# Attention with 16 heads: spread maxima in a PSUM bank, one K evicted amid the scores, low halves of the weighted sums on GpSimd

## The reference

```python
B, Tt, D = hidden_states.shape        # 32, 112, 512
scale = HEAD_DIM ** (-0.5)            # HEADS = 16, HEAD_DIM = 32
a = _layer_norm(audio_kv, ln_gamma, ln_beta)
Q = (hidden_states @ Wq.T).reshape(B, Tt, HEADS, HEAD_DIM).transpose(0, 2, 1, 3)
K = (a @ Wk.T).reshape(B, Ta, HEADS, HEAD_DIM).transpose(0, 2, 1, 3)
V = (a @ Wv.T).reshape(B, Ta, HEADS, HEAD_DIM).transpose(0, 2, 1, 3)
scores = jnp.einsum('bhtd,bhsd->bhts', Q, K) * scale
scores = jnp.where(mask, scores, jnp.float32(-jnp.inf))
attn = jax.nn.softmax(scores, axis=-1)
out = jnp.einsum('bhts,bhsd->bhtd', attn, V)
out = out.transpose(0, 2, 1, 3).reshape(B, Tt, D) @ Wo.T
return hidden_states + jnp.tanh(gate) * out
```

## Time and profile before

| | us |
|---|---|
| runs: lowest, median, highest | 1032.9, 1038.71, 1041.41 |
| the profiled execution | 1042.68 |
| its span, first to last instruction | 1040.9 |
| busy: PE / PEld / DVE / ACT / POOL | 963.9 / 823.3 / 939.4 / 698.5 / 635.5 |
| mean granted TensorE clock | 0.970 |

### The profile page before, as it was taken

How to read it: one execution, slowest core, us unless ns; L and a number is a source line. 1 busy time by engine, 2 the same in 40 slices (tenths; PEclk the granted TensorE clock), 3 DMA queues, 4 the chain that set the end, 5 groups by cost and what they waited for, 6 DMA issues and landing times.

```text
span 1040.9 us, 26655 instructions
## 1 busy us (share of the span) xinstructions
PE 963.9 (93%) x10687; PEld 823.3 (79%) x10687; DVE 939.4 (90%) x1446; ACT 698.5 (67%) x1299; POOL 635.5 (61%) x665
## 2 busy tenths in 40 slices
PE   8999999999999999999999999999999999999956
PEld 7888877778787787787878877887787877878744
DVE  6852799999999999999999999999999999999997
ACT  2422767777767777677776777776777777776662
POOL 0943456667666666566766667565676666665554
PEclk9999999999999999999999999999999999999988
DMA  9971333233443344323343334423344433433101
GB/s 293 328 245 72 77 86 80 59 80 100 103 103 83 88 103 101 96 65 93 100 104 103 86 85 100 103 78 89 88 101 102 103 83 89 100 96 81 35 20 52
DMA packets 85851, 105.54 MB, mean 101 GB/s; under 512 B 22528, under 2 KB 63488, under 8 KB 85728
## 3 DMA queue, kind: packets, MB, share of 16 engines
q1 hardware_dynamic: 85152, 102.93, 37.5%
q10 hardware_dynamic: 576, 0.92, 0.3%
HBM read 86.39 MB, written 17.43 MB: 100 GB/s over the span
## 4 chain that ended last, share of the span: by engine, by line
DVE 57%; PE 20%; ACT 10%; issue 10%; DMA 2%; POOL 1%; SPq 0%; ACTq 0%; DVEq 0%; POOLq 0%
DVE shared_q L837 25%; DVE rmax L827 13%; PE banks L931 12%; ACT shared_q L607 7%; DVE spread L818 6%; PE banks L954 5%; DVE top L815 3%; PE banks L1086 2%; DVE spread L847 2%; DVE stats L754 2%; DVE dsum L842 2%; DVE shared_r L856 2%; ACT shared_q L616 1%; DMA shared_q<-in_wvT 1%; ACT shared_f L657 1%
## 5 line engine op out<-in xcount | busy, mean ns | idle before, releaser
L837 DVE TENSOR_TENSOR shared_q<-shared_q,spread 125x448 f32<-125x448 f32 x384 | 359.3, 989 | 4.4
L931 PE MATMUL banks<-shared_r,w_k 128*128 128x376 f32 x1536 | 314.1, 356 | 51.8 <-ACT shared_f L621 51.4
L931 PEld LDWEIGHTS banks<-shared_r,w_k 128*128 128x128 f32 x1536 | 274.7, 198 | 79.6 <-ACT shared_f L621 70.8
L474 POOL TENSOR_TENSOR shared_f<-shared_q 125x448 f32<-125x448 f32 x126 | 160.6, 1275 | 240.3 <-PE banks L1092 219.1
L616 ACT ACTIVATE shared_q<-shared_q 125x448 f32<-125x448 f32 x384 | 209.3, 575 | 122.9 <-DVE shared_q L837 122.6
L931 PE MATMUL banks<-w_v,shared_r 128*125 128x512 f32 x1152 | 288.2, 399 | 0.0
L931 PEld LDWEIGHTS banks<-w_v,shared_r 128*125 128x125 f32 x1152 | 218.1, 190 | 45.9
L607 ACT ACTIVATE shared_q<-banks,maskT,rstd 125x448 f32<-125x448 f32 x384 | 242.8, 728 | 1.9 <-PE banks L1073 1.9
L827 DVE TRANSPOSE_TENSOR_REDUCE rmax<-shared_q 128x14 f32<-128x448 f32 x384 | 210.1, 606 | 24.0 <-ACT shared_q L607 23.4
L478 POOL TENSOR_TENSOR shared_f<-shared_f,shared_q 125x448 f32<-125x448 f32 x126 | 170.3, 1352 | 9.9
L454 POOL TENSOR_TENSOR shared_r<-cn,shared_r 128x375 fp32r<-128x375 f32 x124 | 124.6, 1026 | 72.9 <-ACT shared_r L563 72.9
(11 more groups left out here) (92 smaller groups left out, 743.2 us busy)
## 6 DMA issues: line engine op xcount, KB each, us to landing
cn<-in_ctxT SPq DMA_DIRECT2D x128, 187.5 KB, 3.7
rows<-in_ctx SPq DMA_DIRECT2D x32, 720.0 KB
xy<-in_x SPq DMA_DIRECT2D x32, 224.0 KB, 7.2
q_kept<-shared_q SPq DMA_DIRECT2D x8, 896.0 KB, 5.5
shared_q<-q_kept SPq DMA_DIRECT2D x32, 224.0 KB, 3.9
out<-xy SPq DMA_DIRECT2D x32, 224.0 KB, 3.6
shared_f<-in_xT SPq DMA_DIRECT2D x7, 896.0 KB, 11.2
x<-row_stats SPq DMA_DIRECT2D x64, 84.0 KB
```

The lines of the kernel that those rows point to most:

```text
L474: pool.tensor_tensor(psum[0:SP_, h, :], prob[0:SP_, q, 0, :], prob[0:SP_, q, 1, :], ALU.add).then_inc(sum_half, 1)
L837: dve.tensor_tensor(prob[0:SP_, p % NB, j, :], prob[0:SP_, p % NB, j, :], spread[0:SP_, :], ALU.subtract).then_inc(sub_done, 1)
L931: last = pe.matmul(dst, l, m, start=(start and k == 0), stop=(stop and k == len(pairs) - 1))
```

## The change

Three things are changed, and what they need.

1. `spread`, 448 columns in SBUF, becomes the first 448 columns of PSUM bank 0, one of the banks of the scores. The transpose of the maxima (now L834) writes there and the subtraction (now L853) reads one input from SBUF and one from the bank. The reciprocals get a buffer of their own in SBUF, `rspread`, which also serves the maxima of the last pair but one. Since the scores of a pair overwrite bank 0, the scores of an even slot n now wait also until the subtractions of all slots up to n - 3 are done. In the tail the sums move to other banks.
2. ACT evicts K of slot 2m + 2 between the scores of slot 2m and those of slot 2m + 1, no more behind both.
3. The low half of the weighted sums is formed by POOL, behind the chunk sums of its turn, no more by DVE at the start of its turn.

```diff
-        spread = sb("spread", [128, HT])
+        rspread = sb("rspread", [128, HT])
...
+        spread = bank[0][:, 0:HT]
-        last_bank = {2: (bank[2], bank[3]), 3: (bank[4], bank[5])}
+        last_bank = {2: (bank[3], bank[4]), 3: (bank[5], bank[1])}
...
@@ gpsimd
+            def low_half(b):
+                pool.wait_ge(o_hi, b + 1)
+                pool.tensor_tensor(oT[:, 1, :, :].rearrange("p c t -> p (c t)"),
+                                  pv[:, b % 2 * HT:b % 2 * HT + HT],
+                                  oT[:, 0, :, :].rearrange("p c t -> p (c t)").bitcast(F32),
+                                  ALU.subtract).then_inc(o_done, 1)
...
                     sum_chunks(2 * m - 3)
+                if odd and c > 1:
+                    low_half(c - 2)
...
             result(B - 3)
+            low_half(B - 2)
             add_bias(B - 2)
...
@@ scalar
                     scores_out(2 * m)
+                if pair(m + 1):
+                    k_out(2 * m + 2)
                 if m == PAIRS - 1:
                     exponential(SLOTS - 3)
                 if pair(m):
                     scores_out(2 * m + 1)
                 if pair(m + 1):
-                    k_out(2 * m + 2)
                     first_out(m + 1)
...
@@ vector
+            def maxima_of(p):
+                return rspread[:, :] if p // 2 == PAIRS - 2 else spread
...
-                dve.transpose(spread[:, :].rearrange("p (k a) -> p k a", a=32),
+                dve.transpose(maxima_of(p).rearrange("p (k a) -> p k a", a=32),
                               top[:, :].unsqueeze(2).to_broadcast([128, BLK, 32])) \
                     .then_inc(spread_done, 1)
...
-                                      spread[0:SP_, :], ALU.subtract).then_inc(sub_done, 1)
+                                      maxima_of(p)[0:SP_, :], ALU.subtract).then_inc(sub_done, 1)
...
-                if odd and c > 1:
-                    low_half(c - 2)
                 if odd and c + 2 < B and c + 2 > 2:
                     statistics(c + 2)
...
             normalise(B - 2)
-            low_half(B - 2)
             without_maximum(SLOTS - 2)
...
@@ tensor
                 if n % 2 == 0:
                     need(pe, s_out, n * ST)
+                    need(pe, sub_done, (n - 2) * ST)
...
-            weighted_sums(SLOTS - 6, bank[0])
+            weighted_sums(SLOTS - 6, bank[1])
...
-            weighted_sums(SLOTS - 4, bank[1])
+            weighted_sums(SLOTS - 4, bank[2])
             output(B - 2, B * ST)
             last_weighted_sums(SLOTS - 2)
+            pe.wait_ge(pv_out, SLOTS - KT)
             last_weighted_sums(SLOTS - 1)
```

More of the change, by code:

```diff
@@ L713, in _ @@
             v_out(B - 1, 2)
-            weighted_out(SLOTS - 6, 0)
+            weighted_out(SLOTS - 6, 1)
             gated_out(B - 3, KB)
             high_half(B - 2)
-            weighted_out(SLOTS - 4, 1)
+            weighted_out(SLOTS - 4, 2)
             exponential(SLOTS - 2)
@@ L846, in normalise @@
                 dve.wait_ge(rden_done, b + 1)
-                dve.transpose(spread[:, :].rearrange("p (k a) -> p k a", a=32),
+                dve.transpose(rspread[:, :].rearrange("p (k a) -> p k a", a=32),
                               rden[:, :].unsqueeze(2).to_broadcast([128, BLK, 32])) \
@@ L851, in normalise @@
                 o = pv[:, b % 2 * HT:b % 2 * HT + HT]
[L852 to L859, removed]
+                dve.tensor_tensor(o, o, rspread[:, :], ALU.mult).then_inc(o_norm, 1)
             def last_divide(k):
```

## The result

The changed kernel takes 960.0 us (median of four runs, 958.6 to 962.5), the kernel before beside it 1036.7 (the 1038.7 of the table above is the median of three of these four runs). The ratio is 0.926, 95% interval 0.921 to 0.931: 7.4% faster. The profiled execution took 960.5 us.

What follows compares the result with a forecast made beforehand. DVE (95% busy) and PE (94%) were taken as nearly full, PE's floor limiting the gain. From 1042.7 us, 52 for the steady part (14.41 to 13.55 a pair) and 5 at the end gave 985.7; named 985, range 965 to 1015.

Steps and rivals of the forecast that it cites:

- 1.70 us for three with a bank: DVE's subtractions: three take 1.70 us with maxima in PSUM, giving back 131 us of DVE in the steady part.
- the low half at nothing in the steady part: Low half moved from DVE to POOL: costed at nothing in the steady part; 40 us if POOL's cover were gone.
- the loop at 12.8 us: Steady loop from a pair's scores through ACT and DVE to its last subtraction: 12.8 us, against PE's return at 12.91.
- the end at 5 us: Kernel's end, last subtractions and pair 63's exponentials: 5 us gained, bounds 2 and 8.
- The sum's middle part, the new wait: PE's scores wait for DVE's subtractions of two pairs before; loop nearly ties with PE, 0.3 us a pair lost.
- The 65 ns estimated from the Trainium skill: DVE subtractions reading PSUM: each 65 ns dearer, 0.4 us a pair, making the sum about 15 us more.
- PE's floor: PE's steady pace without its wait for the K eviction: 13.25 us a pair, trusted to 0.1 us.
- second derivation: PE's pace from the timeline: 12.91 us at full clock plus 0.43 for half-clock stretches, 13.34 a pair.
- PE's granted clock as before, 0.97: Expected sign in the changed kernel's profile: PE's clock stays 0.97; were it lower, the floor would be wrong.
- The 0.3 us for the tie: Loss from delays where DVE's 12.8 us loop nearly equals PE's 12.91: 0.3 us a pair, between 0 and 0.6.
- PE's floor is reached: Rival for the steady part: PE sets the pace, 13.25 us a pair, 967 us in all; chance 0.12.
- The slower rival: Subtractions stay contended, so the new wait rules the loop: 14.8 us a pair, 1067 us; chance 0.08.

Runs made afterwards that it cites:

- kout_alone: The kernel before with only the K eviction moved between the two slots' scores; 998.9 us, ratio 0.962.
- after_sbuf: The changed kernel with the spread maxima in an SBUF buffer of their own, the new wait of the scores kept; 1123.3 us, ratio 1.076.
- before_fill: The kernel before with eight useless matmuls on PE ahead of each batch's first V projection from batch 3 on; 1021.1 us beside 1041.4, ratio 0.979.
- before_fill2: The kernel before with two useless matmuls on PE ahead of each batch's first V projection from batch 3 on; 1007.9 us beside 1037.9, ratio 0.974.
- after_stall3: The changed kernel with PE waiting, before even pairs' second K projection from pair 6 on, until the first slot's first tile is subtracted; 1052.0 us.
- after_stall2: The changed kernel with PE waiting for DVE's spread maxima before every pair's second K projection from pair 6 on; 1060.4 us.

## Why the prediction was wrong

**Right.** Both engines nearly full, the subtraction's second SBUF input as what POOL and DVE hinder one another by, 1.70 us for three with a bank (1.68), the transpose into a bank at the old price (660 ns for 645, 0.01 us), the low half at nothing in the steady part, the loop at 12.8 us (12.75), the end at 5 us (5.6). That the early K covers most of PE's wait is so in the kernel before (`kout_alone`: 63.1 us of waits for L621 became 12.6), but with the bank nothing is left for it to cover. The sum's middle part, the new wait, is the one that would have turned the change into a loss without the bank, and `after_sbuf` did so. The 65 ns estimated from the Trainium skill (VectorE: DVE Perf Modes, the errata section), which gives an operation from PSUM more fixed cycles than one from SBUF, did not appear: the subtractions from the bank took 611 to 623 ns, those from SBUF that overlap no POOL instruction 609 to 627.

**The step that failed is PE's floor,** "14.41 - 1.16 = **13.25 us**" and its second derivation, "12.91 + 0.43 = 13.34". Both left in the floor the 0.43 us that the half-clock stretches cost, and I even listed "PE's granted clock as before, 0.97" among what the profile would show, and weighed a lower clock but never a higher one. It was 1.00. These stretches were not a load on PE that stays; they followed the very stalls that the change removes. `before_fill` and `before_fill2` show it from the one side (1.00 and 20 to 30 us less, with stalls filled or shortened), `after_stall3` from the other (0.96, 26 us). That the two derivations agreed was no support, since both took the old clock. The 0.43 is itself a little high, since 0.97 is rounded: between pair 3 and pair 63 the trace has the lower level for 47.8 us, 23.9 us of PE's work, 0.40 a pair.

**Two smaller terms.** The 0.3 us for the tie were not paid (3.4 us of waits in all, 0.06 a pair). The floor at full clock is 13.08, not 12.91, since a K projection that follows V without a stall takes 2.14 for 2.01 and that V 2.73, from its start to K's (650.71 to 653.44), for 2.67. The kernel before hid this in its wait, which is counted from the end of V's weight loads. This 0.17 us is also half of DVE's room in the tie.

In us a pair: 13.55 forecast, - 0.40 (clock) - 0.30 (tie) + 0.17 (K behind V) + 0.06 (between 13.25 and 12.91 + 0.40) = 13.08. Over 60 pairs the clock is 24 us and the tie 18, with 14 the other way from the last two: 28. The start took 3.1 back and the end gave 0.6, so that the miss, 57 forecast against 82, is 25. Of the start, 1.8 us fall to the first pairs, which had been costed at nothing; there the new wait does bind (1.07 and 1.54 us ahead of the scores of pairs 2 and 3).

The rival "PE's floor is reached" (967, chance 0.12) was what happened, with its floor set too high. The slower rival's mechanism was real, as `after_sbuf` shows; its condition (contended subtractions) was not met.

## What to carry to other kernels

A TensorE that is nearly full has two floors: its work at the clock it has now, and its work at the clock it gets when its stalls are gone. Look at what stands ahead of each slow stretch before taking the mean clock over into the new sum. Where DVE and GpSimd both run operations with two inputs in SBUF, moving one small, often read operand of DVE into a part of a PSUM bank helped both here; and the wait that the borrowed bank brings is to be laid out as a loop, since the same wait cost 128 us with slow subtractions and about 3 us with fast ones.

## What the runs showed of the hardware

- A DVE subtraction of 448 columns with one input in a bank: 611 to 623 ns over 378 executions beside a busy POOL; with both inputs in SBUF: up to 1687 ns in the same kernel; in the kernel before 609 to 627 ns where no POOL instruction overlaps it, a median of 1561 ns where one does.
- The granted clock of TensorE followed single stalls at one place: it fell to 1.2 GHz behind 14 of 15 stalls of 2.24 to 2.26 us (kernel before) and behind 18 of 29 of 2.41 us and more (`after_stall3`), while 51 stalls of 1.75 to 2.10 us, 98 us in all, left it at 2.4 GHz (`after_stall2`). At another place, ahead of the scores, it fell behind stalls of 1.96 us (`after_sbuf`). Useless matmuls ahead of such a wait made the kernel 2 to 3% faster.
- By their weight loads, a V projection took 2.73 us up to the start of the K projection that followed without a pause, and that one 2.14; with a wait between them 2.67 and 2.01, the wait not counted. A transpose of 448 columns into a bank took 660 ns, into SBUF 645.
